# The normalised rows of ten norms written by GpSimd instead of VectorE

## The reference

```
def _layernorm(x, eps=1e-05):
    return (x - mean(x)) / sqrt(var(x) + eps)          # over the 256 features

x = x + tanh(g_xattn[0]) * wkv(w, u, _layernorm(x), ctx)          # recurrence over 256 tokens
x = x + tanh(g_ffn[0])   * ternary_ffn(_layernorm(x), gate, up, down)     # 256 -> 1024 -> 256
x = x + tanh(g_xattn[1]) * attention(_layernorm(x), ctx, Wq, Wk, Wv)      # 32 heads of 8, normed q and k
x = x + tanh(g_ffn[1])   * experts(_layernorm(x), ...)    # top 8 of 64 experts, and a shared one
```

## Time and profile before

| | us |
|---|---|
| median of 3 runs (474.26 to 477.09) | 474.47 |
| the profiled execution | 473.05 |
| its span, first to last instruction | 471.3 |
| PE / DVE / ACT / POOL busy | 400.7 / 362.6 / 304.1 / 0.2 |

### The profile page before, as it was taken

One profiled execution on the slowest core, in us unless ns is written; L12 is line 12 of the kernel. 1 busy time (PEld: TensorE's weight loads), 2 busy tenths in 40 slices (PEclk: granted clock), 3 DMA queues, 4 the chain that ended last, 5 costly groups with the idle time before them and its releaser, 6 DMA issues.

```text
span 471.3 us, 7717 instructions
## 1 busy us (share of the span) xinstructions
PE 400.7 (85%) x2609; PEld 194.6 (41%) x2612; DVE 362.6 (77%) x813; ACT 304.1 (65%) x441; POOL 0.2 (0%) x4
## 2 busy tenths in 40 slices
PE   1024758888756899999999999999999999999996
PEld 1011345434432344456643343355444444444443
DVE  5899796855789999799998576689456777777754
ACT  4899876899738645777698788736334444444422
POOL 0000000000000000000000000000000000000000
PEclk9997797899957699999999999999999999999998
DMA  8503214200000345434231654110324555554201
GB/s 289 237 1 112 67 44 125 68 1 1 3 1 33 112 135 168 134 114 124 78 113 57 210 137 125 56 57 2 120 95 147 170 168 171 170 162 130 67 24 45
DMA packets 31778, 47.99 MB, mean 102 GB/s; under 512 B 5626, under 2 KB 15226, under 8 KB 31228
## 3 DMA queue, kind: packets, MB, share of 16 engines
q1 hardware_dynamic: 31740, 47.51, 31.8%
HBM read 46.18 MB, written 1.31 MB: 101 GB/s over the span
## 4 chain that ended last, share of the span: by engine, by line
PE 74%; DVE 16%; issue 5%; ACT 4%; DMA 1%; SPq 0%; DVEq 0%; ACTq 0%
PE ps L1899 37%; PE ps L2235 17%; PE ps L2012 6%; PE ps L2000 3%; PE ps L1890 2%; PE ps L1943 2%; PE ps L2022 2%; PE ps L1924 1%; PE ps L1979 1%; DMA regC<-in_ctxT_dram 1%; PE ps L1988 1%; DVE regF L1394 1%; DVE tiny L1373 1%; DVE bn L1133 1%; ACT regF L799 1%
## 5 line engine op out<-in xcount | busy, mean ns | idle before, releaser
L1899 PE MATMUL ps<-hH,regW 128*128 128x512 f16 x248 | 84.1, 395 | 6.3 <-ACT regW L1024 3.6
L1024 ACT ACTIVATE regW<-ps 128x512 f32<-128x512 f32 x52 | 31.0, 597 | 85.9 <-PE ps L1899 83.7
L1899 PE MATMUL ps<-hH,regC 128*128 128x512 f16 x264 | 85.5, 379 | 0.0
L1797 DVE TENSOR_TENSOR regW<-ps,regW 128x512 f32<-128x512 f32 x64 | 44.1, 689 | 44.0 <-PE ps L1899 43.6
L1899 PE MATMUL ps<-hL,regC 128*128 128x512 f16 x132 | 50.0, 379 | 0.0
L1899 PE MATMUL ps<-hL,regW 128*128 128x512 f16 x124 | 49.0, 395 | 0.0
L2235 PE MATMUL ps<-regW,regC 128*128 128x512 f16 x198 | 48.2, 379 | 0.5 <-DVE regW L1780 0.5
L1037 ACT CAST regW<-regW 128x512 f16<-128x512 f32 x64 | 39.2, 612 | 9.7 <-DVE regW L1824 5.2
L2235 PE MATMUL ps<-regW 128*128 128x512 f16 x180 | 45.1, 388 | 0.2 <-DVE regW L1780 0.2
L1780 DVE TENSOR_TENSOR regW<-regW 128x512 f16<-128x512 f32 x64 | 43.7, 683 | 1.1 <-ACT regW L1037 1.1
L1899 PEld LDWEIGHTS ps<-hH,regW 128*128 128x128 f16 x248 | 25.0, 101 | 40.9 <-issue 6.6
(11 more groups left out here) (249 smaller groups left out, 699.9 us busy)
## 6 DMA issues: line engine op xcount, KB each, us to landing
regW<-routing_dram SPq DMA_DIRECT2D x130, 128.0 KB, 2.9
regP<-in_gu_dram SPq DMA_DIRECT2D x36, 256.0 KB, 2.9
fw<-in_gu_dram SPq DMA_DIRECT2D x20, 256.0 KB, 3.0
regP<-in_dp_dram SPq DMA_DIRECT2D x36, 128.0 KB, 3.0
regO<-in_ffn_dram SPq DMA_DIRECT2D x3, 1024.0 KB, 9.3
fw<-in_dp_dram SPq DMA_DIRECT2D x20, 128.0 KB, 3.1
x<-in_x_dram SPq DMA_DIRECT2D x2, 512.0 KB, 8.3
regC<-in_ctxT_dram SPq DMA_DIRECT2D x1, 1024.0 KB, 5.3
```

The costliest lines, as they stand in the source:

```text
L1024: nc.scalar.activation(sgm[:, c % 2, :], bank(gate_bank(c)), ACT.Silu, scale=UNSCALE).then_inc(esilu_done, 1)
L1797: V.tensor_tensor(rows, bank(gate_bank(c) + 1), rows, ALU.mult).then_inc(et_done, 1)
L1899: mm = T.matmul(out_ap, w(k), a(k), start=(n == 0), stop=(n == 3 * DK - 1))
```

## The change

The rows of the ten norms other than 1 and 7 are written by GpSimd. VectorE's last root step of such a norm counts up a new semaphore `rooted`; GpSimd, in the order of the norms, waits for that count (and, as VectorE did, for the turn of the former rows in the same tiles), then writes the norm's two or four tiles one after another with the same instruction and operands, counting up `xn_ready`. Norms 1 and 7 keep their rows on VectorE. Nothing changes on the other engines or in the written orders; a norm on VectorE is shorter by two or four steps at its end.

```diff
+        rooted = sem("rooted")
+        POOL_NORMS = [q for q in range(12) if q not in FFN_NORMS]
...
             def root_rest(which, q, v, r, t, out, gain):
...
-                post(V.tensor_tensor(out, t, r, ALU.mult), ("root", which, q))
+                ins = V.tensor_tensor(out, t, r, ALU.mult)
+                if which == "norm" and q not in FFN_NORMS:
+                    ins.then_inc(rooted, 1)
+                else:
+                    post(ins, ("root", which, q))
...
             def bits_root(which, q, v, r, t, src, mul, eps, gain):
...
-                post(V.scalar_tensor_tensor(r, t, 1.5 * k, r, ALU.add, ALU.mult), ("root", which, q))
+                ins = V.scalar_tensor_tensor(r, t, 1.5 * k, r, ALU.add, ALU.mult)
+                if which == "norm" and q not in FFN_NORMS:
+                    ins.then_inc(rooted, 1)
+                else:
+                    post(ins, ("root", which, q))
...
             def norm(q):
...
-                for t in range(a, b):
-                    after(("root", "norm", q))
-                    if q in FORMER:
+                if q in FFN_NORMS:
+                    for t in range(a, b):
+                        after(("root", "norm", q))
                         dve.wait_ge(xn_turned, FORMER[q] + 1)
-                    ins = V.tensor_scalar(xn[:, t, :], x[:, t, :], mv[:, t, 0:1], out[:, t - a:t - a + 1],
-                                          ALU.subtract, ALU.mult)
-                    if q in FFN_NORMS:
-                        post(ins, ("xn", q, t))
-                    else:
-                        ins.then_inc(xn_ready, 1)
-                    yield
+                        post(V.tensor_scalar(xn[:, t, :], x[:, t, :], mv[:, t, 0:1], out[:, t - a:t - a + 1],
+                                             ALU.subtract, ALU.mult), ("xn", q, t))
+                        yield
...
+        @block.gpsimd
+        def _(pool):
+
+            def norm_rows(q):
+                a, b = NORM_TILES[q]
+                inv = norm_set[:, q % 4, 3, :]
+                pool.wait_ge(rooted, POOL_NORMS.index(q) + 1)
+                if q in FORMER:
+                    pool.wait_ge(xn_turned, FORMER[q] + 1)
+                for t in range(a, b):
+                    nc.gpsimd.tensor_scalar(xn[:, t, :], x[:, t, :], mv[:, t, 0:1], inv[:, t - a:t - a + 1],
+                                            ALU.subtract, ALU.mult).then_inc(xn_ready, 1)
+
+            for q in POOL_NORMS:
+                norm_rows(q)
```

## The result

The change takes 499.44 us (median of 4 runs, 498.17 to 500.1) where the kernel before takes 474.37 beside it: ratio 1.0521, interval [1.0486, 1.0556], 25.1 us more. The forecast was 475.6, its range ended at 480.5, and even the rival with slow rows had 482.4. Slower by more than 1% had a chance of 0.22; a loss of this size had none of its own.

The account below looks back on a forecast made before the run. TensorE was taken to bound the kernel (74% of the chain), VectorE's time counting only where TensorE waits. Terms -0.1 + 0.2 + 0.3 + 0.3 - 0.4 + 0.8 = +1.1 us on the median 474.47 gave 475.6, range 472.4 to 480.5.

Parts of the forecast that it names:

- Price of a row on GpSimd: Time r of one 128x256 row on GpSimd: taken as 0.6 us, between 0.41 and 0.95, rows one after another.
- norm 0: Four rows, with turns and copies ending near 12.2, before VectorE's scan at 12.77: hidden, 0.5 us to spare.
- norm 3: Rows on GpSimd come earlier than on busy VectorE, so the second pair of turns gains 0.1 us.
- norm 4: TensorE wants the second row before GpSimd ends it: +0.2 us with the hand-over, passed on by ScalarE and VectorE.
- norm 5: TensorE already waits here; the turns and the router's logits behind them come later: +0.3 us.
- norm 8: TensorE wants the second row before GpSimd ends it: +0.3 us; VectorE's freed time gains nothing.
- norm 9: Rows between query and key norm steps; VectorE can go on at once, a gain of 0.4 us.
- norms 10 and 11: Four rows in line on GpSimd delay turns, logits and routing: +0.8 us, the largest term.
- the hand-over: GpSimd starts an estimated 0.1 us after VectorE's first row started; passing rows on to TensorE stays as before.
- rival A: Two-input VectorE passes and GpSimd rows keep each other out, at norms 0, 3, 8 to 11: +4.0 us, 478.5; chance 0.24.
- rival C: Relief of VectorE: eight freed rows in its two full stretches count in full, 3.3 us faster, 471.2; chance 0.10.
- Rival B: Slow GpSimd rows: loss passes 1% from about 0.8 us a row; 482.4 at 0.95; chance 0.11.

Follow-up runs that it names:

- the filled kernel: The change, plus identity transposes on TensorE ahead of the rows of all GpSimd's norms but 0; 491.65 us, ratio 1.0371 to the kernel before.
- the copies: The change with each of its 24 GpSimd rows a plain copy of x; 474.79 us, ratio 1.0019 to the kernel before.
- the last rows with filler: The kernel before with only the last row of the ten norms on GpSimd and identity transposes on TensorE ahead of norms 3 and 5; 476.91 us, ratio 1.0048.

## Why the prediction was wrong

**The step that failed is "Price of a row on GpSimd".** It took 0.6 us and called 0.95 the upper end; it is 1.22. Both ends came from other engines: the lower from VectorE, the upper from a VectorE pass over three times the columns, the value from ScalarE. No row showed GpSimd doing arithmetic, the text said so, and then used them as if they were bounds. The Trainium skill's GPSIMD Engine Reference, in Elementwise — side-by-side cycle accounting, has 1.8 cycles an element at 1.2 GHz as the best case, an estimate of 0.38 us for 256 elements without the dispatch; the trace disagrees by a factor of three for this form, and a copy is near it (0.40). With r = 1.22 the prediction's own steps give: norm 0 +1.9, norm 2 +0.5, norm 3 +1.1, norm 4 +1.4, norm 5 +1.6, norm 6 +2.1, norm 8 +1.6, norm 9 +0.8, norms 10 and 11 +3.3, together +14.3. So the price alone takes a forecast of next to no change to 489. The remaining 10.8 of the measured 25.1 us is what the steps lacked, two things of which the runs show: rows that are held, and TensorE's lower clock. The estimated 0.1 us of the hand-over was not at fault: at norm 0 the root's last step ended at 7.72 and GpSimd began at 7.82.

Stage by stage, from the starts of the same instructions in the traces of before and after (the first high half behind a norm, or the next tile's statistics); the last mark is the span's end:

| from the mark before | to | in the change, us | the steps at 1.22 us |
|---|---|---|---|
| start | scans behind norm 0 | 2.7 | 1.9 |
| | statistics for norm 2 | 2.4 | 0 |
| | high half of norm 3 | 2.2 | 1.6 |
| | statistics for norm 4 | 1.7 | 0 |
| | high half of norm 4 | 1.4 | 1.4 |
| | high half of norm 5 | 1.6 | 1.6 |
| | statistics behind norm 6 | 2.4 | 2.1 |
| | high half of norm 8 | 1.7 | 1.6 |
| | statistics for norm 10 | 4.2 | 0.8 |
| | high half of norm 10, then the end | 1.5 + 4.8 | 3.3 |

From norm 4 to norm 8 the steps are right within 0.3 us each: there the same working, with the right price, would have served. The other places differ.

*Norms 0, 3 and 9.* Rows are held. GpSimd's 24 rows take 32.7 us and not 24 times 1.22 = 29.3: 3.4 us are holds, 1.36 at norm 0 beside the low half of the context, 0.5 at norm 3 and 1.6 at norm 9. Norm 9's two rows in the change, with VectorE's passes beside them:

```profile
248.22 4.02 POOL L1876 TENSOR_SCALAR xn<-x,mv,norm 128x256 f32<-128x256 f32 x2 [7.74 <-DVE norm L1124]
248.34 0.69 DVE L1318 TENSOR_TENSOR kc<-kc,rows 128x512 f32<-128x512 f32 x1
...
252.30 0.69 PE L1912 MATMUL ps<-identf,xn 128*128 128x128 f32 x2 [1.84 <-POOL xn L1876]
```

This is rival A, half of it. The Trainium skill's SBUF — State Buffer, in Who interferes with whom, has whoever comes second blocked fully. The trace agrees for GpSimd's rows; for VectorE it does not, whose passes begun during a row grew by 0.0 to 0.2 us.

At the price of 0.61, which the prediction took, rival A was the better forecast: it said 478.5, 4.0 above the median, where the forecast's steps have 1.3, and the kernel with such rows lost 3.9 (2.6 to 5.2). So leaving the holds at nothing was a second mistake. By the marks of the table above this kernel lost 0.2 and 0.3 us at norms 4 and 5 (A: 0.2 and 0.3), 1.0 at norm 8 (1.2), 0.3 at norm 9 (0.3) and 1.4 at norms 10 and 11 (1.5): at norms 8 to 11 that is 2.7 us in place of the forecast's 0.7. Only norm 0 misses (nothing, A 0.5), and 1.0 behind norm 3 is in neither. Its rows of norm 8, two in 1.91 us in place of 1.18, and its four of norms 10 and 11 show the holds, and with this operation VectorE is held too, a small step 0.55 us in place of 0.15:

```profile
227.26 1.91 POOL L1876 TENSOR_TENSOR xn<-x 128x256 f32<-128x256 f32 x2 [85.51 <-DVE norm L1124]
...
324.94 2.84 POOL L1876 TENSOR_TENSOR xn<-x 128x256 f32<-128x256 f32 x4 [86.42 <-DVE norm L1124]
325.01 0.55 DVE L1124 SCALAR_TENSOR_TENSOR norm<-norm 128x2 f32<-128x2 f32 x1
```

*Behind norm 3, behind norm 9 and behind norms 10 and 11* TensorE ran at the lower clock: the statistics for norm 4 come 1.7 us later although no row stands between. Windows that hold the same work behind norm 3, in the kernel before, in the change, and in the kernel with only norms 10 and 11 on GpSimd (the granted clock is the number behind POOL's):

```profile
85.00:91.00 6.00, 4.67 (x58) 2.70 (x56) 5.72 (x12) 4.39 (x7) 0.00 (x0) 0.88 0.26 70
```

```profile
92.20:99.87 7.67, 6.60 (x57) 3.32 (x56) 5.90 (x12) 4.74 (x7) 0.00 (x0) 0.60 0.34 101
```

```profile
87.71:94.89 7.18, 6.12 (x58) 3.40 (x56) 5.90 (x12) 4.35 (x7) 0.00 (x0) 0.66 0.33 88
```

The third kernel has norm 3's rows on VectorE, at the same wait as before, and yet 0.66 and 1.2 us more: here the lower clock comes without slow rows too, and 1.2 of the 1.7 us are not shown to be the change's. Behind norms 10 and 11 it came in the change and not in the kernel before; behind norm 9 it came in the change (0.58 from 252 to 256 us) but not in the kernel with only norms 8 and 9. By the marks of the table the filled kernel is shorter than the change by 2.4 us behind norm 3, 0.4 behind norm 6, 1.5 behind norm 9 and 3.1 behind norms 10 and 11, together 7.3, close to the 7 of the ratio; 0.7 of it the same turns also bring to the kernel before. The steps at 1.22 (14.3), the holds (3.4) and the clock (7) make 24.7 of 25.1; that the three add up so well is in part luck, since they were measured in different kernels and some holds are hidden.

*The feed-forward stage* (the second line of the table) lost 2.4 us in the profile with no norm in it that moved. This I do not put down to the change. The same stage in two kernels that do the same work up to its end, the kernel before and the one with filler turns at norms 3 and 5 only:

```profile
40.00:67.00 27.00, 15.98 (x87) 8.68 (x88) 23.85 (x53) 22.03 (x29) 0.00 (x0) 0.81 0.19 59
```

```profile
40.00:69.40 29.40, 18.24 (x88) 9.88 (x88) 24.04 (x53) 22.00 (x29) 0.00 (x0) 0.77 0.18 54
```

It comes in two lengths, 2.4 us apart, by itself. Of the sixteen traces four have the short kind: the kernel before, the filled change, the copies, and the last rows with filler; among the twelve of the long kind are six with norm 0's rows on VectorE. The profile of before happened to be of the short kind and that of the change of the long kind, so the spans differ by 26.5 where the medians differ by 25.1. What chooses the length is open.

*What was right*: that the row is a link and not a load. Relief of VectorE (rival C) brought nothing at any price, not even with rows of 0.40 us. That norms 10 and 11 would be the largest term holds in the table too (6.3 us), though alone on GpSimd they cost no more than norms 8 and 9 (4.7 each). Rival B had the right cause, slow rows, and a chance of 0.11 because its price was capped.

## What to carry to other kernels

Before work moves to an engine that does nothing in the trace, its price has no bound from above by rows of other engines; say so, and let the range reach well past them (here the price was twice the one taken and 1.3 times the upper end), or measure one instruction first. Ask of a moved instruction who waits for it before asking who is relieved: here 9.8 us of VectorE's time were worth nothing and 0.8 us on each link were worth 25. And count a wait at TensorE higher than its length where TensorE sets the pace behind it, as behind norms 10 and 11 here.

## What the runs showed of the hardware

- GpSimd's price depends on the operation as well as on the shape. For 128x256 in float32: copy 0.40 us, product of a tensor with itself 0.61 (of two pieces of one, on 252 columns, 0.72), one operation with one operand per partition 0.92, two operations with two 1.22 (with two constants, on 255 columns, 1.09). VectorE does the two with two in 0.41.
- Between GpSimd and VectorE the holds fall mostly on GpSimd: a row of 1.22 us took up to 2.58 beside a long pass of VectorE, while that pass took 2.40 in place of 2.29. The most that a VectorE instruction lost was about 0.4 us, beside GpSimd's passes of 512 columns (small steps of the root, 0.56 in place of 0.16) and beside the products of 0.61 us, where five of 18 lost 0.33 to 0.42.
- TensorE's granted clock was 0.50 for 5 us behind three waits of 0.7 to 0.8 us with short turns between; transposes of the identity in these gaps kept it at 1.00 (339 to 344 us of that kernel), and the six matmuls behind them took 1.46 us in place of 2.77. Behind norm 3 the clock differed (0.88, 0.66) in two kernels whose rows there are both VectorE's.
- One stage of this kernel, unchanged, takes 27.0 or 29.4 us.
